# Self-attention of a two-layer decoder: three bfloat16 parts read back from DRAM replaced by fp32 operands in SBUF, with a first-pass ring of four single banks

## The reference

```
# layer 0 (no mask): bias, then a LayerNorm over each head's 16 values
q = (x @ Wq + bq).reshape(b, s, NH, HD)            # k and v likewise
q = _layernorm(q, q_scale, q_bias)                 # k and v likewise
scores = jnp.einsum('bqhd,bkhd->bhqk', q, k) * scale
probs = jax.nn.softmax(scores, axis=-1)
out = jnp.einsum('bhqk,bkhd->bqhd', probs, v).reshape(b, s, NH * HD)
return out @ Wo + bo
# layer 1 (causal)
qkv = (x @ qkv_w + qkv_b).reshape(b, s, 3, h, hd)
logits = jnp.einsum('bqhd,bkhd->bhqk', q, k)
logits = jnp.where(causal_mask, -jnp.inf, logits) * scale
att = jax.nn.softmax(logits, axis=-1)
```

## Time and profile before

| | us |
|---|---|
| median of 3 runs | 2077.92 (2072.51 to 2078.95) |
| span of the profiled execution | 2074.9 |
| until the first fill of layer 0 | 140.0 |
| attention of layer 0, to `project` | 140.0 to 605.7 |
| `qkv1` of layer 1 starts | 1187.1 |
| attention of layer 1, to `project` | 1251.8 to 1580.9 |

### The profile page before, as it was taken

One profiled execution on the slowest core, in us unless ns is written; L12 is line 12 of the kernel. 1 busy time (PEld: TensorE's weight loads), 2 busy tenths in 40 slices (PEclk: granted clock), 3 DMA queues, 4 the chain that ended last, 5 costly groups with the idle time before them and its releaser, 6 DMA issues. The chain is left out here.

```text
span 2074.9 us, 30519 instructions
## 1 busy us (share of the span) xinstructions
PE 1461.4 (70%) x8446; PEld 757.8 (37%) x8447; DVE 1322.2 (64%) x5100; ACT 835.9 (40%) x1658; POOL 371.6 (18%) x274
## 2 busy tenths in 40 slices
PE   4769998998983344434365366988998884369994
PEld 2432222222233333323243232434435673136662
DVE  6989787887528999999841466776753457601112
ACT  2732666666763322222231240655565553111110
POOL 2760000000003222223302351000000332210003
PEclk9966999999997777777677695999999997679997
DMA  7184232221000000000014258224400022651003
GB/s 245 61 200 64 35 43 43 32 40 17 24 1 1 1 1 1 1 1 1 1 44 137 64 159 161 42 42 67 58 2 1 9 39 36 218 175 31 30 20 91
DMA packets 122611, 116.29 MB, mean 56 GB/s; under 512 B 47010, under 2 KB 95966, under 8 KB 122468
## 3 DMA queue, kind: packets, MB, share of 16 engines
q1 hardware_dynamic: 116087, 103.12, 22.5%
q0 software_dynamic: 3072, 8.39, 1.3%
q10 hardware_dynamic: 3312, 3.02, 0.4%
HBM read 72.74 MB, written 41.49 MB: 55 GB/s over the span
## 5 line engine op out<-in xcount | busy, mean ns | idle before, releaser
L1016 DVE TENSOR_REDUCE arena<-banks 128x1 f32<-128x512 f32 (+1 forms) x896 | 514.5, 627 | 163.1 <-PE banks L872 86.8
L976 ACT ACTIVATE arena<-banks 128x512 f32<-128x512 f32 (+3 forms) x896 | 430.1, 557 | 325.1 <-PE banks L889 180.6
L872 PE MATMUL banks<-arena 96*128 96x512 bf16 (+1 forms) x896 | 334.4, 397 | 39.8 <-DMA arena<-v 20.2
L889 PE MATMUL banks<-arena 98*128 98x512 bf16 (+3 forms) x896 | 291.1, 367 | 11.0 <-ACT arena L976 5.1
L1209 PE MATMUL banks<-arena 128*77 128x128 f32 x512 | 86.2, 324 | 213.8 <-POOL arena L1332 207.6
L1322 POOL TENSOR_TENSOR arena<-arena 128x1232 f32<-128x1232 f32 x48 | 108.7, 2265 | 693.4 <-DVE arena L1382 434.1
L906 PE MATMUL banks<-arena 128*32 128x512 f32 (+3 forms) x1792 | 219.0, 564 | 16.7 <-ACT arena L976 12.8
L1370 DVE MATCH_REPLACE8 arena<-arena 128x77 f32<-128x77 f32 x1024 | 213.7, 224 | 0.0
L872 PEld LDWEIGHTS banks<-arena 96*128 96x128 bf16 x896 | 86.3, 100 | 268.3 <-DVE arena L1016 174.2
L1864 DVE COPY arena<-banks 128x1024 f32<-128x1024 f32 x23 | 28.2, 1224 | 205.0 <-PE banks L1803 205.0
L1209 PEld LDWEIGHTS banks<-arena 128*77 128x77 f32 x512 | 74.4, 181 | 225.1 <-POOL arena L1332 211.1
(11 more groups left out here) (214 smaller groups left out, 2019.1 us busy)
## 6 DMA issues: line engine op xcount, KB each, us to landing
arena<-parts SPq DMA_DIRECT2D x192, 128.0 KB, 7.1
arena<-in_L_ffn_W SPq DMA_DIRECT2D x16, 1024.0 KB, 12.0
parts<-arena SPq DMA_DIRECT2D x24, 512.0 KB, 8.4
v<-arena SPq DMA_DIRECT2D x32, 256.0 KB, 2.3
arena<-v SPq DMA_DIRECT2D x16, 512.0 KB, 10.5
arena<-sorted SPq DMA_DIRECT2D x46, 128.0 KB, 2.1
sorted<-arena SPq DMA_DIRECT2D x10, 512.0 KB, 9.2
expert_out<-arena ACTq DMA_DIRECT2D x23, 128.0 KB, 2.4
```

The lines of the kernel that those rows point to most:

```text
L872: mm = pe.matmul(PS[:, f % NBK, 0:w], qst[r][0:KS, j, i * P:(i + 1) * P], kst[r][0:KS, j, kb * BANK:kb * BANK + w], start=True, stop=not diag)
L889: mm = pe.matmul(bank, kst[r][0:KM, j, kt * P:(kt + 1) * P], qst[r][0:KM, j, c0:c1], start=True, stop=not diag)
L976: act.activation(prob[(kt * G + j) % PR][:, c0:c1], PS[:, NBK + n % NBK, 0:c1 - c0], ACT.Exp, scale=SCALE).then_inc(sem(s + "_exp"), 1 if ...
L1016: dve.tensor_reduce(m2[:, j, i, kb:kb + 1], PS[:, f % NBK, 0:w], AX.X, ALU.max).then_inc(sem(s + "_red"), 1)
```

## The change

- Queries and keys stay in SBUF as fp32. Head j of a unit lies in partitions 32j to 32j+15, with one more row for the maximum (`KM` is 17). A product of scores (`scores` L776, `second_pass` L816) reads 16 or 17 rows, fp32, starting at partition 32j. The split, the stores to DRAM and the loads back are gone.
- The first pass has four banks (`n % 4`), each filled for one head and reduced by one DVE instruction; heads alternate fastest. The turned maxima and the turned outputs go through the same ring as entries of their own (`MAX`, `OUT`). The second pass keeps three banks (`4 + n % 3`). `ring` and `upto` write out how many ring entries stand ahead of each product of the second pass.
- `weighted` (L828) sums one half of the queries (512) per group, into one bank (7), one group of four heads for each tile of 128 keys: 16 groups in a unit of layer 0, 12 in one of layer 1.
- The causal mask is still a product of `identb` by `future` or `futureT` (L779, L819), all 128 rows, after the 16-row product in the same bank.
- `qkv0` adds the bias by a product with `first_row`, reads projections from PSUM, pads each head to 32 columns, and turns 8 blocks of 128 instead of 4. `qkv1` makes q and k padded to 32 per head: 32 chunks of 512 columns instead of 16.
- `prepare_cross` is cut in pieces (`turned`, `copied`, `blocked`, `valued`) that are called between the first fills of layer 0, with the copies on ACT and the products of masks on POOL instead of DVE. The maxima go by four DMAs instead of one. Attention is unrolled.

```diff
-QUERY_PARTS = (0, 0, 0, 1, 1, 2)
-KEY_PARTS = (0, 1, 2, 0, 1, 0)
+KM = HD + 1
+AHEAD = 16
...
+                    for n0, nw in ((0, BANK), (BANK, 3 * D - BANK)):
+                        for k in range(KD):
+                            pe.matmul(dst, hT[:, k, i * P:(i + 1) * P], w_qkv0[:, k, n0:n0 + nw], start=(k == 0), stop=False)
+                        mm = pe.matmul(dst, first_row, w_qkv0[:, 2, n0:n0 + nw], start=False, stop=True)
...
-                        mm = pe.matmul(PS[:, f % NBK, 0:w], qst[r][0:KS, j, i * P:(i + 1) * P],
-                                       kst[r][0:KS, j, kb * BANK:kb * BANK + w], start=True, stop=not diag)
+                    row = slice(SLOT * j, SLOT * j + HD)
+                    bank = PS[:, n % 4, :]
+                    mm = pe.matmul(bank[:, 0:w], queries(u)[row, i * P:(i + 1) * P], keys[row, u, kb * BANK:kb * BANK + w],
+                                   start=True, stop=not diag)
+                    if diag:
+                        mm = pe.matmul(bank[:, w - P:w], identb, future, start=False, stop=True)
...
+                    while done[0] < upto:
+                        n = done[0]
+                        kind, u, f = ring[n]
+                        if n >= 4:
+                            pe.wait_ge(sem(s + "_red"), n - 3)
...
+                    row = slice(SLOT * j, SLOT * j + KM)
+                    if n >= 3:
+                        pe.wait_ge(sem(s + "_exp"), n - 2)
+                    bank = PS[:, 4 + n % 3, 0:BANK - lo]
+                    mm = pe.matmul(bank, keys[row, u, kt * P:(kt + 1) * P], queries(u)[row, half * BANK + lo:(half + 1) * BANK],
+                                   start=True, stop=not diag)
+                    if diag:
+                        mm = pe.matmul(bank[:, 0:P], identb, futureT, start=False, stop=True)
...
+                for n in range(first_due):
+                    first_pass(n + 1)
+                    if aside:
+                        aside[0](pe, n)
...
+                        for j in range(G):
+                            first_pass(upto[u][gi * G + j])
+                            second_pass(u, gi, j)
+                            if j == 1 and gi:
+                                weighted(u, gi - 1)
+                            elif j == 1 and u:
+                                weighted(u - 1, NGR - 1)
```

More of the change, by code:

```diff
@@ L75, in fills, with key_groups @@
         for k in range(0, keys, BANK):
-            out.append((i, k // BANK, min(BANK, keys - k)))
+            for j in range(G):
+                out.append((i, k // BANK, j, min(BANK, keys - k)))
+    return out
+def key_groups(causal):
+    out = []
+    for half in range(S // BANK):
+        for kt in range(TB):
+            lo = max(0, kt * P - half * BANK) if causal else 0
+            if lo < BANK:
+                out.append((half, kt, lo))
     return out
@@ L378, in prepare_cross, with values @@
-            return turn
+                if n >= 2:
+                    pe.wait_ge(sem("kt"), n - 1)
+                for k in range(KD):
+                    mm = pe.matmul(PS[:, 4 + n % 2, 0:B * C], xw_t[2 * l][:, k, half * P:(half + 1) * P],
+                                   ctxT[:, k, :], start=(k == 0), stop=(k == KD - 1))
+                mm.then_inc(sem("kt_ps"), 1)
+            def values(pe, n):
+                l, b = n // B, n % B
+                if n >= 2:
+                    pe.wait_ge(sem("vx"), n - 1)
+                for k in range(KD):
+                    mm = pe.matmul(PS[0:C, 6 + n % 2, 0:D], ctxT[:, k, b * C:(b + 1) * C],
+                                   xw_t[2 * l + 1][:, k, :], start=(k == 0), stop=(k == KD - 1))
+                mm.then_inc(sem("vx_ps"), 1)
@@ L381, in lgT @@
+            return turned, copied, blocked, valued
         def lgT(l):
@@ L729, in dest @@
-            def dest(i, n):
-                b, m, half = where(i)
-                return parts[b][:, n, m, half * BANK:(half + 1) * BANK]
-            act_split, second_rest, third_rest = split_chunks(s, u_bufs, source, dest)
+            (first, own), keys, values = heads_of()
+            chunks = [(b, g, qk, half) for b in range(B) for g in range(NG) for qk in range(2) for half in range(S // BANK)]
+            NCH = len(chunks)
+            def dest(i):
+                b, g, qk, half = chunks[i]
+                unit = keys[:, b * NG + g] if qk else (first, own)[b][:, g]
+                return unit[:, half * BANK:(half + 1) * BANK]
@@ L956, in _, with weighted @@
-                with pe.Fori(0, 2) as i:
-                    for r in range(NST):
-                        unit((i, r))
-                unit((2, 0), units_left=1)
-                unit((2, 1), units_left=0)
-                turn_output((2, 1))
+                def weighted(u, gi):
+                    half, kt, lo = groups[gi]
+                    pe.wait_ge(sem(s + "_exp"), (u * NGR + gi + 1) * G)
+                    if kt == 0 and (u or half):
+                        pe.wait_ge(sem(s + "_o"), 2 * u + half)
+                    for j in range(G):
+                        mm = pe.matmul(PS[SLOT * j:SLOT * (j + 1), 7, lo:BANK], values[:, u // NG * TB + kt, u % NG * G + j, :],
+                                       prob[:, gi % 2 * G + j, lo:BANK], start=(kt == 0), stop=(gi == last_of[half]))
+                    mm.then_inc(sem(s + "_pv"), 1)
```

1004 lines of the change are left out of this document (430 added, 574 removed).

## The result

The changed kernel takes 3600.8 us (median of 4 runs, 3600.0 to 3603.8) against 2078.4 us before (2072.5 to 2083.5): 1.733 times as long, 95% interval 1.730 to 1.737. I had forecast 2520 us with a range up to 2960. The direction was right, the size was not.

The account below looks back on a forecast made before the run. PE was taken to set each unit's time. Added costs of 148 us in layer 0 and 295 in layer 1 on 2074.9, and 3, gave 2521, stated as 2520 us, with a range from 2340 to 2960.

Parts of the forecast that it names:

- one rival only: Layer 1 attention: the clock falls to 1.2 GHz, a unit takes 129 us, the whole 2956; chance 10%.
- the drains: PE, each change of product shape: 0.10 us each way, so 0.20 us per masked score in layer 1.
- A unit of layer 0: Layer 0 attention: 9 groups of 4.70 and 7 of 3.82 us, plus 3, make 72 us against 52.5.
- same-head group: Layer 0, group whose fill and second-pass product share a head: first product starts 0.88 us late, group takes 4.70 us.
- one a head ahead: Layer 0, group whose fill is one head ahead: the first second-pass product starts at once, group takes 3.82 us.
- strict order: Rival, layer 0: products start strictly in program order, same-head group 5.6 us, unit 79, whole 2570; chance 20%.
- row groups do not overlap: Rival, score products: heads' products run one after another, group 8.2 us, layer 0 unit 135, whole 3130; chance 11%.
- The full overlap: Score products: four heads' fp32 products run beside each other, 0.88 us for four instead of 3.5.
- A unit of layer 1: Layer 1 attention: 64 masked scores 52 us, plain ones 10, sums 7.7 and 3.0, turns 2: 75 against 36.5.
- `qkv0`: Layer 0 projections: PE needs 4.75 us a tile, DVE and ACT less; done at 115.4 us instead of 140.0.
- Start of layer 0: First fill to second pass: 16 lone fills drained both sides plus prepare_cross 32 us, 64 fills 38.4; 70.6 in all.
- The ends: Layer 1's `qkv1`: 69 us instead of 41, but the 23 us from there to the first fill go.

Follow-up runs that it names:

- e1: The changed kernel with score products reading all 32 rows of their head's group instead of 16 and 17: 3213.3 us.
- e2: The kernel before, its bfloat16 score products cut from 96 and 98 rows to the first 16 in both passes: 2616.1 us.
- e4: The changed kernel with score products reading all 128 rows, so the scores of the four heads are added up: 3033.0 us.
- e7: The kernel of e1 (32 rows per score product) without the two mask products of layer 1: 2485.3 us.
- e13: The kernel of e11 with the sum of values one pair later, behind product 2 of the next group instead of product 1: 2277.0 us.
- e9: The kernel of e5 with the causal mask moved off TensorE; GpSimd zeroes the future half of diagonal probability tiles: 2469.6 us.
- e14: The kernel of e11 with two thrown-away products of 128 rows by 512 columns behind each sum of layer 1: 2366.9 us.
- e5: The kernel of e1 with the next unit's first pass one fill further ahead (AHEAD 17 instead of 16): 3122.7 us.
- e6: The changed kernel (16 rows) without the two mask products of layer 1: 3060.8 us.
- e12: The kernel of e5 with eight thrown-away products of 128 rows by 512 columns behind each sum of layer 1: 3057.8 us.
- e8: The changed kernel with ScalarE in qkv0 copying q and k of tile i-3 out before squaring tile i: 3562.0 us.
- e10: The kernel of e5 with the sixteen pieces of prepare_cross in sets of four behind every fourth fill: 3068.9 us.
- e11: e5's 32 rows and further-ahead fills, plus GpSimd mask, ScalarE copies before the square in qkv0, and prepare_cross pieces in fours: 2395.5 us.

## Why the prediction was wrong

**The step that failed** is the one that gave every product its price at 2.4 GHz and let the clock fall in one rival only, in layer 1, at 10%. I had a row that speaks against it in hand (0.50 with PE busy for 46.7 of 50 us) and read it only as saying that long records do not hold the clock. It was a warning, though not of the same thing: its products read 96 rows, and came one by one at VectorE's pace, 64 in 38.4 us. e1, e2 and e4 show what it was here: the same program with 16, 32 and 128 rows a product has the clock at 0.51, 1.00 and 1.00 in the units of layer 0, and the kernel before falls from 0.98 to 0.52 when its products are cut to 16 rows. In layer 1 only 128 rows, or 32 without the mask products, had it at 0.98 or more through the full units (e4, e7, e13). The rival's own time, 2956, was still too low: it left layer 0 at 2.4 GHz, and its masked unit at 1.2 GHz was 129 us where 146.0 were measured, since it kept the drains at 0.20 us a masked score at that clock too. Doubling my whole units comes closer, by luck in part: 2 x 75 = 150 against 146.0 in layer 1, and 2 x 72 = 144 against 130.5 in layer 0, where I take the waits for ScalarE as what does not scale.

The Trainium skill, TensorE: Matmul & The Clock Gate, Part 1, says that the clock depends on how busy PE has been, and names idle gaps as what costs it. The trace does not agree if busy is the engine's share of time: 970 of 970 us at 0.50. On gaps e9 and e13 are in line with the Trainium skill, since the clock came back where PE was idle for less; but e1 and e14 kept it with as large a share of idle time, so gaps are not the whole of it.

**A unit of layer 0: right, at the clock it was priced for.** Row groups overlap, a same-head group takes 4.71 us at 2.4 GHz (4.70), one a head ahead 3.90 (3.82), a unit 74.0 (72). The fourth product waits 0.66 us for the exponential. The rivals "strict order" and "row groups do not overlap" fall by the same rows and by e5. The full overlap had been taken over from groups of columns, without a row for groups of rows; it came true. Four beside each other take 509.43 - 508.47 = 0.96 us instead of 0.88 in my sum.

By that the Trainium skill's rule of strict program order (the same page, Part 3) does not hold for the starts of products in different row groups here: in the changed kernel four fills start within 0.04 us past products of the second pass that wait. The 3.07 times that the Trainium skill gives there for four row groups is lower than what these fp32 products come to, 3.44 / 0.96 = 3.6.

**A unit of layer 1: the mechanism right but for the clock, the size at 2.4 GHz not shown.** The mask's cost, the largest term, is shown by e6 against the changed kernel (69.7 us a unit). 146.0 us at 0.50 would be 73 us if all of it scaled, and I had 75; but not all of it does. e12 had the clock at 1.00 only in pieces, and there a masked fill of 384 columns cost 1.00 us, not the 0.93 of my sum and not half of 1.79. With 0.10 us more (1.00 less half of 1.79) for each of 64 masked scores the unit would be about 80 us, an estimate from these rows. So the drain, 0.10 us each way from the earlier trace rows, was priced somewhat low for this pair.

**`qkv0`: the term was mis-sized by 53 us.** I counted PE's work, 4.75 us a tile, and wrote that ScalarE and VectorE are shorter than that. The work is 4.75 (e8), but ScalarE's order kept PE waiting: tiles came every 7.49 us, or 9.2 where the clock fell. I had not followed which copy the turns wait for and what stands ahead of it. Putting it right is worth 46 us in that stretch, dips of the clock included: with full tiles at 4.75 us e8 has 1.00 throughout 60 to 110.

**Start of layer 0: 103.3 against 70.6.** The mechanism (each lone fill stands by itself between full products) is right, as e10 shows: in sets of four the stretch is 35 us shorter. 1.2 GHz makes a lone fill 2.0 us instead of 1.08. The four banks of fills add some: of 2.85 us for four maxima, 0.37 were waits.

**The ends** were right: 69.1 us for `qkv1` (69), 495 us behind attention (494 before). For the four DMAs of the maxima PE and its weight load waited 8.6 us in four waits in the whole run, where my sum has nothing for them.

**Where the time went:** in round figures, 46 us are ScalarE's order in `qkv0`; of the 1025 us in the starts and units of both layers, the clock is most. In layer 0 that is shown: of the 58.5 us that a unit is above my 72, e1 takes off 56.5. In layer 1 it is argued: no run has a masked unit of row groups at 2.4 GHz throughout, and by the estimate above the clock is 66 of the 71 us over my 75. With full products at 1.00 the same unit takes 81.3 us (e4).

What stays open: which runs of these kernels keep the clock in the last unit of layer 0 (71 or 92 to 94 us with the same code), what a masked unit takes at 2.4 GHz throughout, and whether the waits or the place of the sum gave e13 its clock.

## What to carry to other kernels

Price a product twice, at either clock, and ask how many of the array's rows it has at work before choosing: six parts stacked to 96 bfloat16 rows looked wasteful next to 16 fp32 rows, but they kept the clock, needed no drain between a score and its mask, and took 0.22 us a product of 512 columns instead of 0.86. A mask as a full product between products of row groups makes the groups take turns, 1.09 us each here; put it on an idle engine, and give the wait for it a step of cover. Where two engines hand tiles to and fro, write out each engine's own order for one tile before calling the shorter one hidden.

## What the runs showed that I had not expected

- Reading 32 rows instead of 16, the added ones zeros, made the kernel 387 us shorter (e1): the clock went from 0.51 to 1.00 in the units of layer 0.
- Products that are thrown away can pay for themselves: 96 more in a unit, and the unit went from 141.4 to 136.5 us (e12).
- A full product on PE's way, 128 rows in place of 16, left the unit of layer 0 as long as it was (130.0 against 130.5 us, e4) and made that of layer 1 65 us shorter.
- Waits of 8.4 us in 410 for GpSimd, 29.3 us of idle time in all, went with a clock of 0.78 (e9); with the sum one pair later the units of layer 1 went from 53.2 us on average (e11) to 44.7 (e13).
